# One product of 64 rows for a head's scores in place of two of 32, in a four-layer transformer kernel

## The reference

```python
scores = einsum('bhnd,bhsd->bhns', q, k) * HD ** -0.5     # HD = 16
o = einsum('bhns,bhsd->bhnd', softmax(scores), v)
```

## Time and profile before

| | |
|---|---|
| time, median of 3 runs | 2662.75 us (2662.02 to 2663.56) |
| the profiled execution | 2661.28 us |
| its span in the profile | 2659.5 us |
| PE busy | 2507.8 us, 94% |
| DVE, ACT, POOL busy | 69%, 48%, 17% |
| DMA engines busy, the main queue | 23.4% |

### The profile page before, as it was taken

The page is one execution under the profiler, slowest core; times in us unless marked ns, Lnnn a source line. Parts: engine busy times, 40 slices in busy tenths (PEclk is TensorE's granted clock), DMA queues, the critical chain, the costliest instruction groups (busy, mean ns, idle before and its releaser), DMA issues.

```text
span 2659.5 us, 66182 instructions
## 1 busy us (share of the span) xinstructions
PE 2507.8 (94%) x27522; PEld 1874.0 (70%) x27522; DVE 1826.8 (69%) x3543; ACT 1269.4 (48%) x1810; POOL 453.0 (17%) x461
## 2 busy tenths in 40 slices
PE   5778999999999999999999999999999999999988
PEld 5556676767777776767677777777777777777766
DVE  4466677777777777776666677777777777777752
ACT  0324554444544445545455545455454544545443
POOL 0011111112111111111111111121212112111111
PEclk7789999999999999999999999999999999999999
DMA  5222222222222222222121222222222221222201
GB/s 185 101 79 72 80 75 78 78 84 73 71 71 68 81 71 83 80 91 89 66 75 50 85 64 74 75 75 88 66 97 88 78 83 61 87 68 78 83 29 39
DMA packets 236652, 207.55 MB, mean 78 GB/s; under 512 B 87634, under 2 KB 221972, under 8 KB 236356
## 3 DMA queue, kind: packets, MB, share of 16 engines
q1 hardware_dynamic: 236356, 203.32, 23.4%
HBM read 58.34 MB, written 4.39 MB: 24 GB/s over the span
## 4 chain that ended last, share of the span: by engine, by line
PE 80%; DVE 12%; issue 4%; ACT 3%; DMA 1%; SPq 1%; POOL 0%; POOLq 0%; DVEq 0%; ACTq 0%
PE ring L1237 11%; PE o_acc L1215 11%; PE ring L1125 10%; PE ring L1246 9%; PE score L1163 8%; PE score L1185 8%; PE ring L1227 7%; DVE row_max_F L861 5%; PE ring L1024 5%; PE score L1190 3%; PE ring L1144 2%; ACT probs L997 2%; PE ring L1147 2%; PE ring L1133 2%; DVE row_max_G L861 2%
## 5 line engine op out<-in xcount | busy, mean ns | idle before, releaser
L997 ACT ACTIVATE probs<-score 120x2048 f32<-120x2048 f32 (+1 forms) x320 | 601.6, 1880 | 365.0 <-PE score L1190 353.9
L861 DVE TENSOR_REDUCE row_max_F<-score 128x8 f32<-128x2048 f32 x192 | 437.8, 2280 | 81.1 <-PE score L1163 81.1
L1237 PE MATMUL ring<-x_t_E,w_fc 128*128 128x256 f32 x1536 | 374.6, 390 | 0.5 <-DVE gated_E L915 0.5
L1246 PE MATMUL ring<-w_fc,h_t 128*128 128x256 f32 x1536 | 369.1, 387 | 1.0 <-ACT h_t L1008 1.0
L861 DVE TENSOR_REDUCE row_max_G<-score 128x16 f32<-128x1920 f32 x128 | 276.0, 2156 | 90.0 <-PE score L1163 89.9
L1008 ACT ACTIVATE h_t<-ring,cols 128x256 f32<-128x256 f32 x384 | 161.2, 471 | 369.8 <-PE ring L1237 369.8
L1237 PEld LDWEIGHTS ring<-x_t_E,w_fc 128*128 128x128 f32 x1536 | 278.6, 189 | 66.8 <-issue 18.7
L1246 PEld LDWEIGHTS ring<-w_fc,h_t 128*128 128x128 f32 x1536 | 283.8, 191 | 58.5 <-issue 19.1
L744 DVE SCALAR_TENSOR_TENSOR q_parts<-ring,cols,q_parts 128x256 fp32r<-128x256 f32 x224 | 97.5, 476 | 183.4 <-ACT q_parts L979 183.3
L1215 PE MATMUL o_acc<-probs,v_self 128*17 128x256 f32 x3072 | 204.1, 383 | 0.0
L1163 PE MATMUL score<-k_F,q_F 32*128 32x256 f32 x3072 | 145.5, 306 | 56.8 <-DVE row_max_F L861 48.2
(11 more groups left out here) (134 smaller groups left out, 3802.6 us busy)
## 6 DMA issues: line engine op xcount, KB each, us to landing
q_G<-q_parts SPq DMA_DIRECT2D x256, 128.0 KB, 2.1
q_F<-q_parts SPq DMA_DIRECT2D x192, 128.0 KB, 2.1
k_F<-k_parts SPq DMA_DIRECT2D x96, 256.0 KB, 2.4
k_F<-k_parts SPq DMA_DIRECT2D x192, 128.0 KB, 2.1
k_G<-k_parts SPq DMA_DIRECT2D x128, 120.0 KB, 2.1
k_G<-k_parts SPq DMA_DIRECT2D x256, 60.0 KB, 1.9
gate_now_P<-gate_rows SPq DMA_DIRECT2D x48, 256.0 KB, 3.6
gate_now_E<-gate_rows SPq DMA_DIRECT2D x48, 256.0 KB, 3.8
```

The costliest lines, as they stand in the source:

```text
L861: nc.vector.tensor_reduce(dst, src, AX.X, ALU.max).then_inc(row_max_ready[r].sem, 1)
L997: nc.scalar.activation(probs[v % 2][0:keys, :, :], score[0:keys, :].rearrange("p (h q) -> p h q", h=2 * GROUPS), ACT.Exp, scale=SCALE).the ...
L1237: last = mm(ps[:, c % 2 * NT:(c % 2 + 1) * NT], w_fc1[:, k, c * P:(c + 1) * P], x_t[r][:, k, :], start=k == 0, stop=k == KC - 1)
L1246: last = mm(ps[:, 0:D], h_t[:, k, t * P:(t + 1) * P], w_fc2[:, k, :], start=k == 0, stop=k == MC - 1)
```

## The change

A head's score becomes one product of 64 rows: 16 features by the four pairs of parts (high-high, high-low, low-high, low-low). Two heads stand side by side, in partitions 0 to 63 and 64 to 127, instead of four; a step issues half as many score products, and the `sel` products stay at 32 rows. In a `T` step each half is now four products of 64 rows and four `sel` products of 32 rows.

To be laid so, `q_parts` is first written to DRAM (`q_way`) and from there read four times; K is written (`k_way`) and read twice. SP waits for the write before it issues the reads. ACT may write the next parts once the write to DRAM has landed. The buffers grow, so others are given up: `w_raw` and the reordering of weights go, `k_G` and `v_ctx` have two buffers instead of three, `gate_now["P"]` one, `x_hat` of `P` and `E` are one buffer, `gated` of `A` and `E` too. `P.gld`, `P.RES` and the MLP norm's `e.LN` change their places in the turn for it, and POOL adds the MLP's two halves one by one. In the diff lines that are only "..." stand for what is left out.

```diff
 F.S0 f.PV3 f.O1 E.H0
-F.S1 E.H1 P.V P.RES
+F.S1 E.H1 P.V
 F.S2 E.H2 P.LN
-F.S3 F.X E.H3 A.PR
+F.S3 F.X E.H3 A.PR P.gld
 G.S0 F.M B.PR R.C E.RES
 G.S1 G.X E.F20a E.F20b R.N
 F.T0 G.M P.Q R.A R.RES e.N
-F.T1 F.PV0 P.K e.A
+F.T1 P.RES F.PV0 P.K e.A
 G.T0 F.PV1 F.O0 R.LN e.LN p.N
 G.T1 G.PV0 G.O0 E.F21a p.A c.NC
 F.T2 G.PV1 G.O1 R.Q c.AC
 F.T3 F.PV2 R.KV E.F21b
-P.ld c.ld P.gld E.gld P.ST
+P.ld c.ld E.gld P.ST
...
-F.S1 P.V P.LN P.RES
+F.S1 P.V P.LN
...
-1G.S0 F.M A.PR 1R.C E.RES
+1G.S0 F.M A.PR P.gld 1R.C E.RES
...
-F.T0 1G.PV1 1G.O1 E.F21b G.M p.N
-F.T1 F.PV0 1R.Q p.A
+F.T0 1G.PV1 1G.O1 E.F21b e.LN G.M p.N
+F.T1 P.RES F.PV0 1R.Q p.A
...
-WORD_AHEAD = {"P.ld": 3, "c.ld": 1, "1R.ld": -3, "P.gld": 1, "E.gld": -3, "P.V": 0, "P.RES": 0, "P.ST": -4}
+WORD_AHEAD = {"P.ld": 3, "c.ld": 1, "1R.ld": -3, "P.gld": 0, "E.gld": -3, "P.V": 0, "P.RES": 0, "P.ST": -4}
...
-        w_raw = sb("w_raw", [P, KC, 2 * D])
...
-        gate_now = {r: [sb(f"gate_now_{r}{i}", [P, 2, D]) for i in range(b)] for r, b in (("P", 2), ("E", 1))}
+        gate_now = {r: [sb(f"gate_now_{r}{i}", [P, 2, D]) for i in range(b)] for r, b in (("P", 1), ("E", 1))}
...
+        x_hat["E"] = x_hat["P"]
...
-        q = {r: [sb(f"q_{r}{i}", [P, KC, 2, NT]) for i in range(2)] for r in "FG"}
-        k_two = {"F": [sb(f"k_F{i}", [P, 2, KC, 2, NT]) for i in range(2)],
-                 "G": [sb(f"k_G{i}", [P, 2, KC, 2, S]) for i in range(3)]}
+        q = {r: [sb(f"q_{r}{i}", [P, 4, KC, NT]) for i in range(2)] for r in "FG"}
+        keys_in = {"F": NT, "G": S}
+        k_four = {r: [sb(f"k_{r}{i}", [P, 4, KC, keys_in[r]]) for i in range(2)] for r in "FG"}
 
         q_parts = sb("q_parts", [P, 2, KC, NT])
         k_parts = sb("k_parts", [P, 2, KC, NT])
-        v_one = {"F": [sb("v_self", [P, TT, H, HD + 1])], "G": [sb(f"v_ctx{i}", [P, H, HD + 1]) for i in range(3)]}
+        q_way = {r: [nc.dram_tensor(f"q_way_{r}{i}", [P, 2, KC, NT], F32, kind="Internal").ap() for i in range(2)]
+                 for r in "FG"}
+        k_way = {r: [nc.dram_tensor(f"k_way_{r}{i}", [P, 2, KC, keys_in[r]], F32, kind="Internal").ap()
+                     for i in range(2)] for r in "FG"}
+        v_one = {"F": [sb("v_self", [P, TT, H, HD + 1])], "G": [sb(f"v_ctx{i}", [P, H, HD + 1]) for i in range(2)]}
...
-        gated = {r: sb(f"gated_{r}", [P, TT, D]) for r in "AE"}
+        gated = sb("gated", [P, TT, D])
...
             def lay_q(r, m, n):
+                at = q_jobs.index((r, m, n))
+                way, q_now = buffer(q_way, r, m, n), buffer(q, r, m, n)
                 sp.wait_ge(q_parts_ready[r].sem, q_parts_ready[r].after(m, n))
+
+                same = [i for i in range(at) if q_jobs[i][0] == r]
+                if len(same) >= 2:
+                    sp.wait_ge(q_laid, 64 * (same[-2] + 1))
+                sp.dma_start(way, q_parts[:, :, :, :]).then_inc(q_on_way, 16)
+                sp.wait_ge(q_on_way, 16 * (at + 1))
                 t_psum[r].wait_before(sp, m, n, len(q[r]))
-                q_now = buffer(q, r, m, n)
-                for e in range(2):
-                    for part in range(2):
-                        sp.dma_start(q_now[part:P:2, :, e, :], q_parts[e:P:2, part, :, :]).then_inc(q_laid, 16)
+
+                src = way.rearrange("(e d) i c n -> d i e (c n)", e=4)
+                for i in range(4):
+                    sp.dma_start(q_now[i:P:4, :, :, :].rearrange("p e c n -> p e (c n)"), src[:, i % 2, :, :])                        .then_inc(q_laid, 16)
 
             def lay_k(r, m, n):
+                at = k_jobs.index((r, m, n))
+                way, k_now, width = buffer(k_way, r, m, n), buffer(k_four, r, m, n), keys_in[r]
                 sp.wait_ge(k_parts_ready[r].sem, k_parts_ready[r].after(m, n))
-                t_psum[r].wait_before(sp, m, n, len(k_two[r]))
-                k_now = buffer(k_two, r, m, n)
-                width = NT if r == "F" else S
-                for e in range(2):
-
-                    sp.dma_start(k_now[0:P:2, :, :, e, :], k_parts[e:P:2, :, :, 0:width]).then_inc(k_laid, 16)
-                    sp.dma_start(k_now[1:P:2, 0, :, e, :], k_parts[e:P:2, 1, :, 0:width]).then_inc(k_laid, 16)
-                    sp.dma_start(k_now[1:P:2, 1, :, e, :], k_parts[e:P:2, 0, :, 0:width]).then_inc(k_laid, 16)
+                same = [i for i in range(at) if k_jobs[i][0] == r]
+                if len(same) >= 2:
+                    sp.wait_ge(k_laid, 32 * (same[-2] + 1))
+                sp.dma_start(way, k_parts[:, :, :, 0:width]).then_inc(k_on_way, 16)
+                sp.wait_ge(k_on_way, 16 * (at + 1))
+                t_psum[r].wait_before(sp, m, n, len(k_four[r]))
+
+                src = way.rearrange("(e d) j c n -> (d j) e (c n)", e=4)
+                for i in range(2):
+                    sp.dma_start(k_now[i:P:2, :, :, :].rearrange("p e c n -> p e (c n)"), src).then_inc(k_laid, 16)
...
-                elif step == "F21b":
-                    pool.wait_ge(gated_ready[r].sem, gated_ready[r].after(m, n))
+                elif step in ("F20b", "F21b"):
+                    t = int(step[2])
+                    pool.wait_ge(gated_ready[r].sem, gated_ready[r].after(m, n, t))
...
+            def gated_added(r, m, n):
+
+                at = gated_jobs.index((r, m, n))
+                if at > 0:
+                    er, em, en = gated_jobs[at - 1]
+                    added = x_mid_ready if er == "A" else x_out_ready
+                    dve.wait_ge(added.sem, added.after(em, en))
...
-                if r == "W" and step != "load":
-                    at = orderings.index((m, step)) + 1
-                    dve.wait_ge(w_raw_loaded, 32 * at)
-                    into = (w_qk,) * 2 if step == "self" else cross_weights(m)[0:2]
-
-                    if FULL_BEFORE[m] > 0 and step == "self":
-                        dve.wait_ge(k_psum.sem, k_psum.after(FULL_LAYERS[FULL_BEFORE[m] - 1], nb - 1))
-                    elif FULL_BEFORE[m] > 0 and FULL[m]:
-                        dve.wait_ge(kv_psum.sem, kv_psum.after(FULL_LAYERS[FULL_BEFORE[m] - 1], nb - 1))
-                    elif m == 1:
-                        dve.wait_ge(mods_psum, LAYERS)
-                        dve.wait_ge(gates_psum, len(FULL_LAYERS))
-                    for i in range(2):
-                        to = i * D if step == "self" else 0
-                        for k in range(KC):
-                            last = nc.vector.tensor_copy(as_ordered(into[i][:, k, to:to + D]),
-                                                         row_order(w_raw[:, k, i * D:(i + 1) * D]))
-                        last.then_inc(w_ordered, 1)
...
-                    ln_psum[r].wait_before(dve, m, n)
+                    if r == "R":
+                        ln_psum[r].wait_before(dve, m, n)
+                    elif hat_jobs.index((r, m, n)) > 0:
+
+                        er, em, en = hat_jobs[hat_jobs.index((r, m, n)) - 1]
+                        dve.wait_ge(ln_psum[er].sem, ln_psum[er].after(em, en))
...
-                        act.wait_ge(laid, 16 * moves * jobs.index((f, m, n)))
+                        act.wait_ge(on_way, 16 * jobs.index((f, m, n)))
...
-                        for e in range(2):
-                            for two in range(2):
-                                for g in range(GROUPS):
-                                    at = slice(32 * g, 32 * (g + 1))
-                                    col0 = g * BANK + (e * NT if r == "F" else (2 * c + e) * S)
-                                    last = mm(score[:, col0:col0 + width],
-                                              q_now[at, c, e, tile * P:(tile + 1) * P].bitcast(F32R),
-                                              k_now[at, two, c, e, :].bitcast(F32R), start=two == 0, stop=two == 1)
+                        for e in range(4):
+                            for g in range(2):
+                                at = slice(64 * g, 64 * (g + 1))
+                                col0 = (2 * g + e // 2) * BANK + (e % 2 * NT if r == "F" else (2 * c + e % 2) * S)
+                                last = mm(score[:, col0:col0 + width],
+                                          q_now[at, e, c, tile * P:(tile + 1) * P].bitcast(F32R),
+                                          k_now[at, e, c, :].bitcast(F32R), start=True, stop=True)
...
-                    for e in range(2):
-                        for two in range(2):
-                            for g in range(GROUPS):
-                                at = slice(32 * g, 32 * (g + 1))
-                                mm(score[0:keys, g * BANK + e * NT:g * BANK + (e + 1) * NT],
-                                   k_now[at, two, c, e, tile * P:tile * P + keys].bitcast(F32R),
-                                   q_now[at, c, e, :].bitcast(F32R), start=two == 0, stop=False)
-                        for g in range(GROUPS):
-                            at = slice(32 * g, 32 * (g + 1))
```

(50 more changed lines are left out.)

73 lines of the change are left out of this document (35 added, 38 removed).

## The result

The changed kernel takes 2865.34 us (median of 4, 2860.51 to 2868.34) against 2662.39 for the one before (2661.53 to 2663.56): ratio 1.0759, 95% interval 1.0746 to 1.0773. It is slower by 203 us. Its profiled execution took 2868.34 us, with a span of 2866.4; the lines used are 1154 (S), 1176 and 1181 (T, `sel`).

A forecast was written before the change was run, and what follows sets the result against it. TensorE was taken as the bound: 2661.3 + 187 (form changes) - 8 - 5 (score rounds) - 5 (waits) + 7 + 1 (laying) - 2 (weight copies) = 2836.3, median 2838 us. Range 2735 to 2880, chance 0.79.

The forecast's parts named there:

- TensorE is the bound, and step distances are the time: Whole kernel: TensorE, busy 94% of the span, sets the time through distances between step starts, not matmul lengths.
- Score products gain nothing: S and T: halved instructions leave the rounds unchanged; only 0.006 us a round saved in `F` and T, none in `G`'s S.
- the term in S: S steps of `F`: 192 steps by four rounds at 0.006 us, a saving of 5 us.
- Changes of form: Inside T: three more changes between 64 and 32 rows, 0.195 us each, over 320 steps: 187 us added.
- The rival of half a change: Inside T: only entry or exit is paid per change, adding 90 to 100 us; about 2745 us; chance 0.12.
- that of no cost between row tiles: Inside T: changes between 64 and 32 rows cost nothing; 2656 us; chance 0.11.
- Laying: Q and K through DRAM: mostly hidden in running turns; +7 us at the start and +1 at the end.
- 5 us later, the second `F` some 2 ... at the end +1: Laying at the start and end: first Q and K 5 us later, second `F` 2, giving +7; the end +1.
- Taken back: TensorE's waits ahead of S steps: longer T steps give DVE and POOL time, recovering 5 us of 69.
- The sum: Whole kernel: 2661.3 + 187 - 8 - 5 - 5 + 7 + 1 - 2 = 2836.3 us; median 2838.
- the -2 for the weight copies: DVE's 28 weight copies and the reordered rows are gone: 2 us saved.
- the rounds: Score rounds of `F` and T: 0.006 us saved each, 8 us in T and 5 us in S.

The follow-up runs named there:

- Two blocks: Changed kernel with all score products of a T step first, then all `sel` products (one change of form inside): 2741.73 us, ratio 1.0291.
- eight blocks: Changed kernel with T split into two 64-row score products, then their two `sel` products, four times (seven changes of form): 3220.42 us, ratio 1.2092.
- the change put into the kernel before: Kernel before, with only T's `sel` products made as 64 rows and two buffers for K of cross-attention: 2923.56 us, ratio 1.0978.
- the detour alone: Kernel before, own layout and products, with Q's and K's parts written to DRAM and read back: 2698.52 us, ratio 1.0130.

## Why the prediction was right

- **TensorE is the bound, and step distances are the time.** It held: 189 us of longer T steps in 207 of span.
- **Score products gain nothing.** Right, and more so than predicted. I took 0.006 us a round from halved instructions (13 us in all, 5 in S and 8 in T). S of `F` stayed at 0.67, to within 0.01 us, so the term in S is 2 us at most; in T it can't be told from the changes of form, and is inside the 189 below. The excess of a round over its stream is not set by the number of instructions. S of `G` stayed at 1.04. That loads of 128 columns pace it is read, not tested; the run with half the products in S gives 0.45 / 4 = 0.11 us a round of 120 columns (the prediction took 0.105), hardly less than the 0.12 of a round of 256, so for `G` the columns streamed don't set it. Two 64-row products do run side by side: one at a time they would add four rounds, and an S step of `F` would take 1.1 us.
- **Changes of form.** The upper bound of 187 us was taken, where no row had 64 beside 32; measured 189. Two blocks (one change), four (three), eight (seven) and the change put into the kernel before fit one account. By T = 0.20 + rounds x 0.115 + changes inside x 0.195 the five T steps are 0.89, 1.09, 1.48, 1.71 and 2.49, measured 0.91, 1.11, 1.51, 1.75 and 2.46 (this one of `G`, the others of `F`). The rival of half a change and that of no cost between row tiles are out. The rule of the Trainium skill (TensorEngine Tiling, Key Properties), that a change of tiling mode drains TensorE, holds between 64 and 32 rows as well, at 0.2 us a change. What the drain consists of is read, not tested: 0.10 of load under no matmul, and 0.09 from the end of the last round to the next load.
- **Laying.** In the middle nothing was late, as predicted. The ends were mis-sized: 8 us predicted, 26 measured (14 and 12). The step that was too low is "5 us later, the second `F` some 2 ... at the end +1". It counted one landing a lay; the write, its reads and the other tensor's write stand in one row on SP. The chain that ended last has it, for the second self-attention:

```profile
82.68 2.82 DMA q_way_F<-q_parts
...
88.10 6.11 DMA k_way_F<-k_parts
...
94.86 5.07 DMA k_F<-k_way_F
100.06 1.22 PE score L1154 x8
```

From Q's parts (82.68) to the S step (100.06) it is 17.4 us. K's write takes 6.1 and its read 5.1. The S step stood at 86.80 before. The landings by group (KB each, median us) against the earlier trace rows: a write of K to DRAM takes twice the time of Q's with the same bytes.

```profile
k_F<-k_way_F SPq DMA_DIRECT2D x96, 512.0 KB, 4.6
...
q_way_F<-q_parts SPq DMA_DIRECT2D x48, 512.0 KB, 2.6
k_way_F<-k_parts SPq DMA_DIRECT2D x48, 512.0 KB, 5.5
```

At the end the same row of lays stands ahead of the last cross-attention. Why K's write takes 5.5 and Q's 2.6 was not tried, but the traces point at what stands ahead of it: in the changed kernel and in that with the detour alone, each of these 48 writes is issued while Q's reads, issued just before it, are still on their way, and the same write lands in 3.5 us where those are four of 128 KB, in 5.5 where they are four of 256 KB. Q's write for `F` has, but for the first, nothing ahead of it. The line of the run with the detour alone:

```profile
k_way_F<-k_parts SPq DMA_DIRECT2D x48, 512.0 KB, 3.5
```

Not all of the 26 is waiting. By the windows, TensorE's idle time (length less busy time of PE) grew by only 5 us in the first and 2 in the last. The other 18 or so are busy time of TensorE beyond the 19 and 9 that longer T steps account for, in stretches whose granted clock fell from 0.87 to 0.85 and from 0.97 to 0.92. As an estimate from these rows, the lower level held for 112 us in place of 88 and for 34 in place of 12, which can cost up to 12 and 11. With the detour alone the idle time grew by 18 and 3 and the busy time by 4 and 4, at 0.85 and 0.95. So the slower laying shows at the ends in two ways, as waits and as a longer time at the lower clock, and longer T steps seem to fill a part of the waits; the shares were not separated.
- **Taken back.** 5 us were predicted, 8 measured in the middle. Most of it is the wait of TensorE for the MLP's norm in turns without layer 1, 24 of them in the middle window. In the kernel before and in the changed one, the distance from the transposes of `R` to those of `E` (whose input is now called `x_hat_P`) is 0.75 and 0.49 us; 24 x 0.26 is 6. The longer T steps give DVE and POOL the time for that norm: the same distance is 0.49 with `sel` of 64 rows in the kernel before, whose T steps are long and whose schedule is the old one, and 0.80 with the schedule and buffers of the change alone.

```profile
1933.68 0.66 PE L1024 MATMUL ring<-ident,x_hat_R 128*128 128x128 f32 x4
1934.43 0.63 PE L1024 MATMUL ring<-ident,x_hat_E 128*128 128x128 f32 x4
```

```profile
1982.37 0.66 PE L1018 MATMUL ring<-ident,x_hat_R 128*128 128x128 f32 x4
1982.86 0.60 PE L1018 MATMUL ring<-ident,x_hat_P 128*128 128x128 f32 x4
```

- **The sum.** Predicted +187 - 13 - 5 + 8 - 2 = +175. Measured +189 - 1 - 8 + 26 = +206, against 206.9 of span; the -2 for the weight copies is not told apart in it. The two errors of sizes, the rounds and the ends, have the same sign, and make most of the 31. The medians are 27 apart (2838 and 2865), because the profiled execution of the changed kernel is 3 us above its median, and that of the kernel before was 1.5 below. So the mechanism and its price were right, and the range held with 15 us to spare, although the ends were too low by a factor of three.

## What to carry to other kernels

Count the changes of the array's form (rows and columns of a product), not the instructions: on this TensorE-bound kernel each cost about the same, 0.2 us, more than a round of products, and the order within a step decides how many there are. Filling idle rows by merging two products of 32 rows into one of 64 brought nothing here, where the narrow ones already ran four abreast, so look at the distance of starts before halving a count. Ask of each product what its result is for: a row maximum that is only a shift can be made from half of the terms, and that gave 3%.

## What the runs showed of the hardware that was not expected

The granted clock fell in mid-run of the kernel with eight blocks, though TensorE was hardly idle: 48.8 of 50 us busy in this window, with a clock of 0.93.

```profile
1500.00:1550.00 50.00, 48.76 (x337) 31.22 (x337) 24.77 (x58) 18.96 (x22) 6.79 (x8) 0.93 0.34 112
```

The timeline of one T step of `G` in it: blocks of 0.50, then 0.34, then 0.31 us (distances of starts).

```profile
1514.75 0.57 PE L1176 MATMUL score<-q_G,k_G 64*120 64x256 f32 x2
1515.25 0.57 PE L1181 MATMUL score<-max_t_G,sel 32*120 32x256 f32 x2
1515.75 0.42 PE L1176 MATMUL score<-q_G,k_G 64*120 64x256 f32 x2
...
1516.40 0.38 PE L1176 MATMUL score<-q_G,k_G 64*120 64x256 f32 x2
```

Ahead of it stood other T steps in eight blocks, in which the array was drained every 0.31 us. The half-rate blocks show the lower of the two levels (1.2 and 2.4 GHz), with 98% of the window busy in the records; the middle windows of the kernel before and of the changed one show 1.00. Over the whole execution the eight blocks have a mean clock of 0.960, the changed kernel 0.974. As an estimate, that is some 110 us more at the lower level, which can cost up to 55; the 25 us over the forecast lie within it, but were not separated.

With three changes a T step no such fall goes with them: the kernel with `sel` of 64 rows, without the detour, has a mean of 0.981, as the kernel before has 0.982. The detour alone has 0.976. So most of the lower clock at the ends of the changed kernel goes with the laying, and little with its changes of form.
